# Four heads and one queue rearranged in an eight-layer transformer chain on one core: the last attention's keys and values made beside the rank counts, and the row writes issued two blocks later

## The reference, cut to what matters

```python
x = x + _L0_xattn_ref(_layernorm(x), ctx, ...)      # A0: 8 heads of 64
x = x + _L0_ffn_ref(_layernorm(x), gate_w, experts) # E0: sinkhorn gates, top-k routing
x = x + _L1_xattn_ref(_layernorm(x), ctx, mask, ...)# C1: one head of 256, masked
x = x + _L1_ffn_ref(_layernorm(x), ...)             # F1: ternary weights, 1024 hidden
x = x + _L2_xattn_ref(_layernorm(x), ctx, ...)      # C2: one head of 256, with biases
x = x + _L2_ffn_ref(_layernorm(x), ...)             # F2: ternary, rms norms, gelu
x = x + _L3_xattn_ref(_layernorm(x), ctx, ctx, mask, ...)  # A3: 16 heads of 16, masked
x = x + _L3_ffn_ref(_layernorm(x), ...)             # F3: 8 experts by position
```

```python
competitive_gates = sinkhorn(gate_logits)           # 8 times: divide by column sums, by row sums
vals, idx = top_k(swapaxes(competitive_gates), M)   # M = N // E = 256 rows of each expert
outputs = einsum('ebmd,edf->ebmf', x[idx], experts) * vals
routed_back = zeros_like(x).at[b_idx, idx].set(outputs)
```

## Time and profile before

| | |
|---|---|
| median of 3 runs | 2703.95 us (2700.22 to 2710.94) |
| the profiled execution, its own time | 2716.91 us |
| its span | 2715.1 us, 32836 instructions |
| PE busy | 2356.1 us (87%) |
| DVE / ACT / POOL busy | 1630.1 (60%) / 1275.1 (47%) / 375.0 (14%) us |
| PE's granted clock by fortieths, the low ones | 6, 6, 6 tenths about 680 to 880 us; 5 about 880 to 950; 5 about 1830 to 1850 |

### The profile page before, as it was taken

One profiled execution on the slowest core, in us unless ns is written; L12 is line 12 of the kernel. 1 busy time (PEld: TensorE's weight loads), 2 busy tenths in 40 slices (PEclk: granted clock), 3 DMA queues, 4 the chain that ended last, 5 costly groups with the idle time before them and its releaser, 6 DMA issues.

```text
span 2715.1 us, 32836 instructions
## 1 busy us (share of the span) xinstructions
PE 2356.1 (87%) x12316; PEld 1227.4 (45%) x12316; DVE 1630.1 (60%) x3448; ACT 1275.1 (47%) x1732; POOL 375.0 (14%) x286
## 2 busy tenths in 40 slices
PE   8999999989555449999988999776999999999788
PEld 3323222222211037777654777562444444444377
DVE  4656666655367734352542453765788867888385
ACT  3554555555166512223522222530577655776753
POOL 0343443433034520000000000000000000000011
PEclk9999999999666568999988999885899988999888
DMA  3000000000130042200101121012110202000131
GB/s 121 5 9 5 9 9 9 9 5 9 47 129 10 14 139 92 88 6 9 53 27 51 61 73 49 5 22 84 47 28 11 34 1 36 7 32 1 61 123 67
DMA packets 63389, 108.33 MB, mean 40 GB/s; under 512 B 13516, under 2 KB 44891, under 8 KB 62203
## 3 DMA queue, kind: packets, MB, share of 16 engines
q1 hardware_dynamic: 61064, 100.85, 12.0%
q0 software_dynamic: 1536, 4.20, 0.5%
q10 hardware_dynamic: 628, 1.14, 0.2%
HBM read 87.88 MB, written 17.74 MB: 39 GB/s over the span
## 4 chain that ended last, share of the span: by engine, by line
PE 52%; DVE 12%; ACT 4%; issue 3%; DMA 3%; POOL 1%; SPq 0%; ACTq 0%; DVEq 0%; POOLq 0%
PE PS L2547 8%; PE PS L1466 7%; PE PS L2528 5%; DVE pm L2656 4%; PE PS L2490 4%; PE PS L1424 2%; PE PS L1447 2%; PE PS L1449 2%; PE PS L1448 2%; ACT dump L1094 1%; DVE ind L1139 1%; PE PS L1248 1%; PE PS L373 1%; PE PS L1257 1%; PE PS L1413 1%
## 5 line engine op out<-in xcount | busy, mean ns | idle before, releaser
L2656 DVE TENSOR_REDUCE pm<-PS 128x1 f32<-128x512 f32 x768 | 478.7, 684 | 101.0 <-PE PS L2490 100.8
L2619 ACT ACTIVATE P<-PS 128x1024 f32<-128x1024 f32 (+1 forms) x416 | 407.1, 1023 | 196.6 <-PE PS L2528 195.1
L2490 PE MATMUL PS<-Ks,Qs 49*128 49x512 f32 x768 | 307.1, 487 | 42.2 <-DMA Qs<-row 26.0
L732 ACT ACTIVATE P<-PS 128x1024 f32<-128x1024 f32 (+1 forms) x208 | 213.2, 1026 | 178.9 <-PE PS L637 167.6
L2528 PE MATMUL PS<-Qs,Ks 51*128 51x512 f32 (+1 forms) x832 | 274.1, 447 | 8.6 <-ACT P L2619 8.6
L650 PE MATMUL PS<-P,V 128*64 128x512 f32 (+1 forms) x832 | 229.0, 629 | 5.8 <-ACT P L732 5.8
L2547 PE MATMUL PS<-P,V 128*17 128x512 f32 (+1 forms) x1664 | 230.2, 626 | 0.3 <-ACT P L2619 0.3
L2528 PEld LDWEIGHTS PS<-Qs,Ks 51*128 51x128 f32 (+1 forms) x832 | 138.8, 190 | 199.7 <-ACT P L2619 145.8
L2490 PEld LDWEIGHTS PS<-Ks,Qs 49*128 49x128 f32 x768 | 135.3, 198 | 133.7 <-DVE pm L2656 89.8
L552 POOL TENSOR_TENSOR odd<-odd,P 128x1024 f32<-128x1024 f32 x64 | 160.1, 2501 | 197.3 <-ACT P L732 197.3
L1032 PE MATMUL PS<-ind,sel 128*8 128x512 bf16 (+3 forms) x288 | 102.2, 474 | 90.7 <-DVE ind L1139 75.9
(11 more groups left out here) (364 smaller groups left out, 4665.2 us busy)
## 6 DMA issues: line engine op xcount, KB each, us to landing
mi<-in_mask SPq DMA_DIRECT2D x32, 800.5 KB, 4.4
We<-in_L_ffn_w SPq DMA_DIRECT2D x16, 1024.0 KB, 7.0
Wg<-gate_rows SPq DMA_DIRECT2D x8, 1024.0 KB, 11.3
Qs<-q_parts SPq DMA_DIRECT2D x90, 64.0 KB, 2.8
Ks<-k_parts SPq DMA_DIRECT2D x24, 200.1 KB, 6.2
R<-denominators SPq DMA_DIRECT2D x32, 128.0 KB, 2.8
q_parts<-T SPq DMA_DIRECT2D x7, 512.0 KB, 2.7
k_parts<-Tk SPq DMA_DIRECT2D x6, 400.0 KB, 2.5
```

The lines of the kernel that those rows point to most:

```text
L732: e.activation(self.P[0:r, n % 4, :, :], PS[0:r, b:b + 2, :], ACT.Exp, scale=0.125).then_inc(*k.ac_exp.up(("A", n)))
L2490: m = e.matmul(PS[:, b, :], self.Qs[rows, s, pr, q0:q0 + 128], self.Ks[rows, s, pr, cs], start=True, stop=not masked)
L2619: e.activation(self.P[0:r, n % 4, :, :], PS[0:r, b:b + 2, :], ACT.Exp, scale=0.25).then_inc(*k.ac_exp.up((3, n)))
L2656: e.tensor_reduce(self.pm[:, u % 2, i, c:c + 1], PS[:, ring.of(("max", key)), :], AX.X, ALU.max).then_inc(*k.dv_max.up((3, *key)))
```

## The change

What the diff does, by stage:

- E0's head: unit 15's reciprocal is taken by DVE from PSUM, in two halves of 256 columns, each followed by the product with On; the DMAs for it go. Three key steps stand ahead of the `wo` products, one behind them, four behind the sinkhorn loop.
- E0's counts: the scatter of `place` becomes a step of its own, `send`, that stands in the list of block t + 2; ACT's part becomes `scaled`. The 21 steps of `L3Keys` stand between the counts (8 keys in t = 5 to 8, 13 values from t = 9), with their weights and results in the dead columns of W.
- E0's experts: loads and conversions of the first four mask tiles, and the 13 value steps of C1, stand in this stage.
- F1: without `L3Keys`; the norm of the last group moves from the first rise to the first fall (in F2 too). C2's weights are loaded at F1's start, its biases at C2's.
- A3: the eight row DMAs are issued by POOL, V's loads wait until the first queries have landed.

```diff
     def weigh_steps(self, t):
-        return ([(self, "turn", (t,))] if t else []) + [(self, "rank", (t,)), (self, "pick", (t,)),
-                                                        (self, "place", (t,))]
+        out = [(self, "send", (t - 2,))] if t > 1 else []
+        out += [(self, "scaled", (t,))] + ([(self, "turn", (t,))] if t else [])
+        return out + [(self, "rank", (t,)), (self, "pick", (t,)), (self, "place", (t,))]
...
-        out += weave((self.att.tail() + sink, 0.0, 1.0), (self.keys.key_steps(), 0.3, 1.0))
+        divide, project, keys = self.att.divide_steps(15), self.att.project_steps(15), self.keys.key_steps()
+        out += divide[:-1] + keys[0:3] + divide[-1:] + project[0:4] + keys[3:4] + project[4:] + sink + keys[4:]
...
+        out = [(self, "fetch", (x,)) for x in range(8)] + mask.load_steps(0, 2) + [(self.keys, "ones", ())]
...
+            if x == 4:
+                out += mask.turn_steps(0, 2) + mask.load_steps(2, 4)
-        out += [(self, "get", (t,)) for t in range(NT)]
+        out += [(self, "get", (t,)) for t in range(NT)] + mask.turn_steps(2, 4) + self.keys.value_steps()
...
+        elif step == "den" and key[0] == 15:
...
+            for half in range(2):
+                cs = slice(256 * half, 256 * half + 256)
+                e.reciprocal(self.R[:, cs], PS[:, b, cs]).then_inc(*k.dv_misc.up(("recip", 15, half)))
+                at.wait_ge(k.dv_misc, ("recip", 15, half))
+                e.tensor_tensor(self.On[:, 1, cs], self.On[:, 1, cs], self.R[:, cs], ALU.mult).then_inc(
+                    *k.dv_misc.up(("On", 15, half)))
...
     def steps(self):
-        return [(self, "part", p) for p in self.parts] + [(self, "value", (kt,)) for kt in range(KT)]
+        out = {(4, 0): [(self, "load", ())], (8, 0): [(self, "value load", ())]}
+        for n, p in enumerate(self.parts):
+            i = 8 * 5 + 4 * n
+            out.setdefault((i // 8, i % 8), []).append((self, "part", p))
+            out.setdefault(((i + 5) // 8, (i + 5) % 8), []).append((self, "low", p))
+        for kt in range(KT):
+            i = 8 * 9 + 4 * kt + 2
+            out.setdefault((i // 8, i % 8), []).append((self, "value", (kt,)))
+        return out
...
-    out = weave((ffn.rise_steps(0), 0.0, 1.0), (norms.steps(norm, 3), 0.0, 1.0))
+    out = ffn.rise_steps(0)
...
-        if qb:
-            parts.append((norms.steps(norm + 1, qb - 1), 0.05, 0.9))
+        parts.append((norms.steps(norm + 1, qb - 1) if qb else norms.steps(norm, 3), 0.05, 0.9))
...
-        out = [(self, "begin", ()), (self, "load", ())] + self.key_loads(0)
-        out += [(self, "part", (0, 0))] + self.query_loads(0, 0) + [(self, "rows load", ()), (self, "value load", ())]
+        out = [(self, "begin", ()), (self, "rows load", ())] + self.key_loads(0)
+        out += [(self, "part", (0, 0))] + self.query_loads(0, 0) + [(self, "value load", ()), (self, "load", ())]
...
         elif step == "value load":
+            at.wait_ge(*self.query_loaded(0, 0))
...
-    keys3 = L3Keys(k, high, ffn1.ring)
-    ffn1.aside = spread(keys3.steps(), 4)
-    out.append(("F1", keys3.load_steps() + ffn1.order()))
+    ffn1.aside = [[]] * 4
+    out.append(("F1", kv2.load_steps() + ffn1.order()))
```

More of the change, by code:

```diff
@@ L520, in sync @@
                     *k.ld_e0.up("all", 16))
-        elif step == "recip":
+        elif step == "recip" and key[0] < 15:
             u, = key
@@ L739, in scalar @@
             e.activation(self.On[:, u % 2, :], PS[:, 6, :], ACT.Copy).then_inc(*k.ac_misc.up(("On", u)))
-        elif step == "den":
+        elif step == "den" and key[0] < 15:
             u, = key
@@ L820, in vector @@
             e.reciprocal(self.Rc[:], self.Rc[:]).then_inc(*k.dv_misc.up(("recip", u)))
-        elif step == "norm":
+        elif step == "norm" and key[0] < 15:
             u, = key
@@ L1075, in scalar @@
                 *k.ac_misc.up(("ccs", t)))
-        elif step == "place":
+        elif step == "scaled":
             t, = key
@@ L1310, in steps, with load_steps, turn_steps @@
         return [(self, "mask", (t,)) for t in range(lo, hi)]
+    def load_steps(self, lo, hi):
+        return [(self, "load", (t,)) for t in range(lo, hi)]
+    def turn_steps(self, lo, hi):
+        return [(self, "turn", (t,)) for t in range(lo, hi)]
     def ready(self, t):
@@ L1316, in sync @@
         t, = key
+        if step == "turn":
+            return
         if t >= self.n:
@@ L1323, in vector @@
         t, = key
+        if step == "load":
+            return
         at.wait_ge(self.ld[t % self.n], t)
@@ L1368, in order @@
         out = [(self, "zero", ())] + list(head)
-        rest = norms.steps(norm, 3) + self.kv.value_steps()
+        rest = norms.steps(norm, 3)
         if self.layer == 2:
-            out += self.kv.key_steps()
+            out += [(self.kv, "ones", ())] + self.kv.key_steps()
+            rest += self.kv.value_steps()
         out += self.query_steps(0) + weave((self.max_steps(0), 0.0, 1.0), (rest, 0.0, 0.9))
@@ L2189, in vector @@
         k, PS = self.k, self.k.PS
-        if step == "part":
+        if step == "low":
             half, c = key
@@ L2465, in gpsimd @@
             e.memset(self.nm[:], 0.0).then_inc(*k.pl_done.up("nm3"))
+        elif step == "rows load":
+            at.wait_ge(k.dv_misc, "row")
+            row, ones = self.row.row[0:1, :].bitcast(F32), self.row.row[32:34, :].bitcast(F32)
+            wide = lambda x, n: x[:, 0:n].unsqueeze(1).to_broadcast([x.shape[0], 4, n])
+            Ks, Qs = (x[:].bitcast(F32).rearrange("p s r n -> p (s r) n") for x in (self.Ks, self.Qs))
+            for o in (48, 112):
+                e.dma_start(Ks[o:o + 1, :, :], wide(row, M)).then_inc(*self.ld_row.up((o, "mask"), 16))
+                e.dma_start(Ks[o + 1:o + 3, :, :], wide(ones, M)).then_inc(*self.ld_row.up((o, "ones"), 16))
+                e.dma_start(Qs[o:o + 1, :, 0:M], wide(ones[0:1, :], M)).then_inc(*self.ld_row.up((o, "q"), 16))
+                e.dma_start(Qs[o:o + 1, :, M:N], wide(ones[0:1, :], N - M)).then_inc(*self.ld_row.up("all", 16))
     def tensor(self, e, at, step, key):
@@ L2943, in stages @@
                            (1, 4, 4, 4), ring2)
-    out.append(("C2", att2.order(kv2.load_steps() + w2.load_steps(), [mask3.steps(4 * qb, 4 * qb + 4) for qb in range(4)])))
+    out.append(("C2", att2.order(kv2.bias_steps() + w2.load_steps(), [mask3.steps(4 * qb, 4 * qb + 4) for qb in range(4)])))
     ks_at, P_at = LOW + 14144, LOW + 54976
```

147 lines of the change are left out of this document (86 added, 61 removed).

## The result

The changed kernel takes 2601.5 us (median of 4 runs, 2596.95 to 2609.98) against 2705.38 for the kernel before in the same session (4 runs, 2700.22 to 2710.94): a ratio of 0.9619, 95% interval 0.9586 to 0.9652. Forecast were 2596 and a range of 2570 to 2640. The profiled execution is the one of 2596.95, with a span of 2595.1.

A forecast was written before the change was run, and what follows sets the result against it. PE, busy 87% of the span, was taken as the bound, with waits where it stands still. Eight terms, 20 + 22 - 3 + 15 + 30 + 8 + 2 + 14 = 108 us, off the 2703.95 median gave 2596, range 2570 to 2640.

The forecast's parts named there:

- E0's head, 20: E0's head: DVE's own reciprocal, keys out of the sum rounds and an earlier gates' trip save 20 us.
- The counts, 22: E0's counts: all 14 DVE waits for POOL go, 39.5 us, less 17.5 for 21 attention steps, leaving 22 us.
- The experts, -3: E0's experts: mask loads between the result writes delay the gather, costing 3 us, bounds 0 and 9.
- C1's head, 15: C1's head: mask conversions and value steps leave it, saving 15 us, 7 to 8 of them the values.
- F1, 30: F1: key and value steps leave, 34 us of PE time; 30 kept because the first rise loses its filler.
- C2's head, 8: C2's head: weights are already there, so of PE's 11.8 us wait 8 us are saved.
- F2, 2: F2's head: ACT's 5.6 us between gelu and the norm's square roots moves to the first fall, saving 2 us.
- A3's head, 14: A3's head: V waits and POOL issues rows, so the first queries' store takes 5 us and 14 us are saved.
- (a): Counts: the last attention's steps cost there what they save in F1, PE becoming the bound; 2618 to 2628, chance 0.20.
- (b): Counts: POOL's scatter stretches beside a busy DVE; 2606 to 2615, chance 0.13.
- (c): More gain than counted: faster clock in blocks 1 to 8, values free, F1 gives all 34; 2580, chance 0.12.
- (d): Slower than before: POOL's scatter bounds every block, the counts losing 100 us; chance 0.02.

The follow-up runs named there:

- the last experiment: Changed kernel with the third and fourth mask load behind the last expert-result write and all eight E0's head keys behind the gates' eight sums: 2595.91 us, ratio 0.9602.
- the scatter in place: Changed kernel with each block's scatter again behind its own place step, not two blocks later; rows still scaled early: 2614.45 us, ratio 0.9674.
- the experiment with the masks behind: Changed kernel with the experts' third and fourth mask load issued behind the last write of expert results: 2606.67 us, ratio 0.9652.
- the experiment on F1: Changed kernel with the last attention's 8 key and 13 value steps made in F1 again: 2625.58 us, ratio 0.9724.
- the kernel with rows scaled late: Changed kernel with the scatter behind its own place step and ACT's scaling back between pick and place: 2645.15 us, ratio 0.9793.

## Why the prediction was right, and where its terms were not

The forecast case came in, with the sum 5.5 us too low. All eight terms have the sign that was forecast, but for F2 that is the clock's doing, and several sizes are right only because errors cancel. By its own steps:

*E0's head, 20: measured 15.9, and 0.6 ahead of it.* DVE's reciprocal takes 1.76 us for 256 columns (I took 1.5, bounds 0.3 and 4), the product starts at 695.2, the four keyless rounds give 9.3 (10). Two steps were mis-sized: the key behind the transposes, moved, gave 1.9 where the sum took 4, and the four keys left took 7.4 us and not 10.5, so that the 4 us I let the block of loads swallow never arose. The first add came 16.5 us earlier and so did that behind the last load of W (771.60 to 755.12). The three keys ahead of the product were not free either: in the last experiment, without them, it starts at 688.1.

*The counts, 22: measured 21.8, by two errors that cancel.* The step "all 14 waits go: 39.5" gave 34.3 (198.7 to 164.4, without the new steps); the 21 steps cost 12.5, not 17.5. (The steps' charge was 21 x 0.85, which is 17.9; I wrote 17.5.) With the waits still there the same steps cost 22.1, so the two parts don't simply add. On the cause the prediction left something out: it put all down to sending two blocks later and never named the scaling, which the change moves too. With the scatter in place that alone takes 33.2 of the 43.9 us. Whether the later sending needs it at all is open, since it was not run with the rows scaled late.

*The experts, -3: measured -5.0.* 3.3 of them stand at the gather, and the experiment with the masks behind gives 1.8 of these back and 1.2 further on. The rest I have not taken apart.

*C1's head, 15: 14.0,* of which the values made 6.8, as said (7 to 8), against 2.1 that they cost in the experts, which I had not charged. The other 7.2 I put down to the masks; no run moves these back. *C1's body, 0: -1.6.* That is the difference between a clock of 1.00 and of 0.99 in it, as above; what sets the clock I haven't found.

*F1, 30: 35.2, and C2's head, 8: 8.1* (11.76 to 3.66). The sum of the steps' own PE time, 34, was the better figure: taking 4 off because the first rise loses its filler was the mistake, since at an equal clock the filler makes 0.1 us. The experiment that moves the steps back gives 37.4. Both numbers hold for a changed F1 at a clock of 0.91. Three other kernels with the same F1 took 118.7 to 119.8 us in it at 0.81 or 0.82, and against these the gain would be 26 to 27.

*F2, 2: 2.7, by luck.* The wait of 5.59 is gone, but one of 5.97 stands in the second rise instead. F2's clock was 0.84 before and 0.89 with the change, and the two kernels that ran it at 0.84 took 124.0 us, one with the norm moved and one with it in its old place. So the step itself, moving the norm, was worth nothing measurable, and the 2.7 us are mostly the clock's.

*A3's head, 14: 7.6, the step that failed most.* I had the store of the first queries land in 5 us once V was out of its way. It took 11.5, and PE's wait was 17.9 us and not near 12: the key stacks and now POOL's rows are ahead of the store. POOL was done with the rows soon, 0.5 to 0.6 us each where I had set 2 as the limit; I had counted its time and not that of the transfers. Holding V back is worth 5.3 and the rows on POOL 2.3 (29.0, 26.7 with V early, 21.4).

*The rivals.* (a) fell with the experiment on F1. (b), POOL stretched beside DVE, cost nothing here: the 16 scatters took

```profile
L1006 POOL DMA_INDIRECT placed_rows<-xs,to x16 | 16.8, 1049 | 11.8 <-DVE rk L1178 6.0 <-POOL Wg L1026 3.9 <-DVE to L1202 1.1
```

1.05 us on the mean, 1.26 at most. But that does not show that a scatter can't be stretched. It is the place in the list that spared them: the first four lay wholly beside the compares that also add up (L1162) and took 1.19, 1.01, 0.99 and 0.98 us, as the first ones did before with DVE waiting (1.18 and 0.99). Four others began while a plain compare (L1160) was still running, for 0.41, 0.34, 0.27 and 0.21 us, and these took 1.26, 1.20, 1.13 and 1.06 us: the longer the overlap, the longer the scatter, by the same amount. The first of them:

```profile
824.51 1.13 DVE L1160 TENSOR_SCALAR ind<-Wg,G 128x1280 bf16<-128x1280 f32 x1
...
825.23 1.26 POOL L1006 DMA_INDIRECT placed_rows<-xs,to  x1 [0.28 <-POOL Wg L1026]
```

With the sending one block later the scatters stood elsewhere in the list and reached 1.57 us, with an overlap of 0.72. By the Trainium skill (SBUF — State Buffer, section "SBUF: two separate sides") DMAs issued from GpSimd starve while DVE runs an instruction that takes both ports. The trace agrees that such a scatter is held up, by the 0.1 to 0.3 us above; no scatter of the changed kernel lay beside a plain compare for its whole length, so the fivefold of the prediction is not tested. The weighing also misread: the median of the 128 adds there is 455 ns, so at least half of them were as short as the eight of block 0, and long ones were not the rule beside DVE. (c), more than counted, came true for F1 alone. (d) and (e) had nothing for them. Of PE's clock the Trainium skill (TensorE: Matmul & The Clock Gate, Part 1) says that idle gaps bring the half rate; the trace agrees, 0.63 in the counts with DVE's waits in them and 0.84 without, though the 21 steps are a part of that (0.72 without waits and without steps).

*The sum against the median, not the profiled time,* was the right choice. Before's profiled execution took 863.0 us in A3 behind its head at a clock of 0.90, those of the thirteen other kernels 842.8 to 857.8, so that is where its 13 us too many seem to lie.

## What to carry to other kernels

When an instruction waits for several engines, look for what stands in front of each producer in its own queue: here moving the cheap producer (ACT's scaling) to the front took 33.2 us out of a stage of 220.8 before the consumer was moved at all. When two moves serve the same wait, four runs are needed to say what each is worth, and here there were three.

PE work taken from a stage in which PE was nearly full (F1) was worth about its full PE time there, 35 us. In a stage in which PE stood idle it cost about a third of that (12.5) with the waits gone, and 22.1 with them.

The store at A3's head took 5.7 or 6.2 us with one kind of transfer issued ahead of it, 11.5 with two and 14.0 with three. Hold back what is not needed first, and count the small transfers too.

A gain of 2 or 3 us in one trace says little. Look for another kernel that ran the same instructions at the same clock: here that turned F2's 2.7 us into nothing.

## What the hardware showed that I had not expected

The granted clock of a stage with the same instructions is not fixed. Kernels whose F1 is identical took 108.0 us in it once (the kernel with rows scaled late), 110.8 (with the change) and 119.8 (with the sending in place); the windows of the first and the last:

```profile
1274.90:1382.80 107.90, 92.72 (x472) 68.97 (x472) 70.95 (x164) 51.44 (x85) 0.00 (x0) 0.94 0.03 8
```

```profile
1239.90:1359.70 119.80, 106.25 (x473) 77.17 (x473) 71.00 (x164) 52.12 (x85) 0.00 (x0) 0.81 0.02 7
```

A3 behind its head, with the same 4740 matmuls, lay between 842.8 and 863.0 us at 0.93 to 0.90. These 20 us are more than any of five of my eight terms, and what sets the clock apart stays open.
